# A three-layer graph attention kernel: layer A in three float32r products, two heads scaled on ScalarE, setup by small products, first and last six turns written out

## What is computed

```python
# layer 0 ("A"), one head of 256
Wh = x @ W;  e = leaky_relu(e_i[:, :, None] + e_j[:, None, :], 0.2)
attention = softmax(where(adj == 0, -1e9, e), axis=2)
x = layernorm(x + elu(attention @ Wh))
# layer 1, first part ("B", four heads of 128) and second part ("C", one head of 256)
mask = (adj > 0) | eye
h = elu(gat(x, mask, W1, att_src1, att_dst1, b1, concat=True))
h = gat(h, mask, W2, att_src2, att_dst2, b2, concat=False)
x = layernorm(x + h)
```

## Time and profile before

| | |
|---|---|
| median of 3 runs | 680.34 us (680.04 to 680.78) |
| the profiled execution | 680.93 us |
| its span, first to last instruction | 679.2 us |
| mean granted TensorE clock | 0.982 |
| busy: PE, DVE, ACT, POOL | 630.1, 598.4, 483.0, 456.0 us |
| bytes moved | 45.81 MB, mean 67 GB/s |

### The profile page before, as it was taken

How to read it: one execution, slowest core, us unless ns; L and a number is a source line. 1 busy time by engine, 2 the same in 40 slices (tenths; PEclk the granted TensorE clock), 3 DMA queues, 4 the chain that set the end, 5 groups by cost and what they waited for, 6 DMA issues and landing times. The chain is left out here.

```text
span 679.2 us, 17442 instructions
## 1 busy us (share of the span) xinstructions
PE 630.1 (93%) x4104; PEld 569.3 (84%) x4104; DVE 598.4 (88%) x2368; ACT 483.0 (71%) x1219; POOL 456.0 (67%) x810
## 2 busy tenths in 40 slices
PE   2468999999999999999999999999999999999883
PEld 1257889998999999889999999998999999999772
DVE  2567899999999999999999999999999999999852
ACT  1226777778777777787777777787777777787651
POOL 0125667777777777677777777777777777777742
PEclk9968999999999999999999999999999999999997
DMA  8112212112222222012222222112222222120000
GB/s 266 29 38 64 64 64 77 51 46 80 78 80 78 64 79 80 30 66 79 80 79 77 66 78 78 38 61 78 80 80 69 72 79 72 37 82 17 18 16 31
DMA packets 46868, 45.81 MB, mean 67 GB/s; under 512 B 2736, under 2 KB 46384, under 8 KB 46768
## 3 DMA queue, kind: packets, MB, share of 16 engines
q1 hardware_dynamic: 43936, 42.48, 19.6%
q10 hardware_dynamic: 2832, 2.23, 1.1%
HBM read 36.31 MB, written 8.39 MB: 66 GB/s over the span
## 5 line engine op out<-in xcount | busy, mean ns | idle before, releaser
L312 POOL TENSOR_SCALAR probB<-probB,rdenB 128x256 f32<-128x256 f32 x256 | 126.1, 505 | 74.3 <-DVE rdenB L618 73.9
L394 ACT ACTIVATE probB<-probB,shiftB 128x256 f32<-128x256 f32 x256 | 127.4, 499 | 24.2 <-DVE shiftB L587 20.7
L845 PE MATMUL PS<-probTB,VB 128*128 128x256 f32 x512 | 127.6, 382 | 0.0
L601 DVE SCALAR_TENSOR_TENSOR probB<-PS,VB,gatedB 128x256 f32<-128x256 f32 x256 | 111.5, 476 | 2.0 <-issue 0.4
L323 POOL TENSOR_TENSOR inlC<-hidT,inhC 128x512 fp32r<-128x512 f32 x64 | 82.2, 1285 | 45.0 <-ACT inhC L450 44.9
L559 DVE CUSTOM_DVE_ANT_0 gatedB<-PS,gate_bc 128x256 f32<-128x256 f32 x256 | 93.0, 417 | 7.7 <-PE PS L815 5.3
L845 PEld LDWEIGHTS PS<-probTB,VB 128*128 128x128 f32 x512 | 90.6, 192 | 8.7
L801 PE MATMUL PS<-WhB,inhB 128*128 128x260 f32 x256 | 81.6, 319 | 2.2 <-DVE inlB L632 2.1
L405 ACT ACTIVATE probTB<-PS 128x512 f32<-128x512 f32 x128 | 72.4, 591 | 8.3 <-PE PS L826 8.3
L294 POOL TENSOR_TENSOR y<-y,xres 128x512 f32<-128x512 f32 x32 | 41.2, 1288 | 51.0 <-DVE y L623 51.0
L801 PE MATMUL PS<-WhC,inhC 128*128 128x258 f32 x256 | 75.1, 293 | 0.2 <-issue 0.2
(11 more groups left out here) (98 smaller groups left out, 1631.7 us busy)
## 6 DMA issues: line engine op xcount, KB each, us to landing
xres<-in_x_dram SPq DMA_DIRECT2D x32, 256.0 KB, 2.7
xTin<-in_x_t_dram SPq DMA_DIRECT2D x32, 256.0 KB, 4.0
adj_in<-in_adj_dram SPq DMA_DIRECT2D x32, 256.0 KB, 4.3
adjT_in<-in_adj_t_dram SPq DMA_DIRECT2D x32, 256.0 KB, 3.1
out_dram<-res SPq DMA_DIRECT2D x32, 256.0 KB, 2.1
WB<-in_L_gnn_W_dram ACTq DMA_DIRECT2D x2, 256.0 KB, 5.8
WC<-in_L_gnn_W_dram ACTq DMA_DIRECT2D x1, 512.0 KB, 11.4
WA<-in_L_gnn_W_dram SPq DMA_DIRECT2D x1, 256.0 KB, 3.0
```

Source lines behind the costliest of these rows:

```text
L312: last = pool.tensor_scalar(B.prob[h][:, k, :], B.prob[h][:, k, :], B.rden[:, k, h:h + 1], 1.0, ALU.mult, ALU.mult)
L394: last = nc.scalar.activation(L.prob[h][:, k, :], L.prob[h][:, k, :], ACT.Exp, bias=L.shift[:, k, h:h + 1], accum_out=den[:, k, h:h + 1] i ...
L601: last = nc.vector.scalar_tensor_tensor(out=L.prob[h][:, k, :], in0=PS[b][:, (h % 2) * N:(h % 2 + 1) * N], scalar=L.V[:, k, h, 1:2], in1=L ...
L845: last = nc.tensor.matmul(PS[b][:, o:o + N], B.V[:, k, h, 2:B.F + 2], B.probT[h][:, k, :], start=(k == 0), stop=(k == NT - 1))
```

## The change

1. **A's projection** uses `project` as B and C do, with `A.Wh`, `A.Wl`, `A.inh`, `A.inl`: `high_a` (ACT) rounds xT, `low_a` (POOL) subtracts. SP's wait for a free xT buffer is on `low_a`.
2. **Heads 2 and 3 of B** are scaled on ACT (`scale_copy`), heads 0 and 1 stay on POOL (`scale`).
3. **Score columns** come from small PE products of the transposed weights, which are laid out and loaded too (`WT`), with two-column vectors (`score_products`), and one DVE copy each. The b1 and b2 rows are loaded once and spread by PE. Broadcast loads and the 28 DVE operations go. The column sums are taken with minus ones.
4. **Setup:** `load_table` (an exp on one element, ACT) and `warm_up` (four 128x128 products, PE) come first; the weight loads lie in the middle of SP's and ACT's lists.
5. **Order:** each queue is a written-out list `fill()`, then `body` for turns 6 to 30 (25 of them), then a written-out list `drain()`. Lags in the body are 0 and 1 for A, 2 to 4 for B, 4 and 5 for C. What a turn contains per batch is the same apart from 1 and 2.

Its core:

```diff
         def iterations(body):
-            for i in range(NB + 5):
+            for i in range(6, NB + 5 - 6):
                 body(Turn(i))
...
             def load_xT(t):
                 if active(t):
                     if t.at >= 2:
-                        for tile in range(NT):
-                            sp.wait_ge(A.s_lin[tile][0], t.this() - 2)
+                        sp.wait_ge(s_loA, t.this() - 2)
...
+            def low_a(t):
+                if active(t):
+                    pool.wait_ge(s_hiA, t.this())
+                    if t.later:
+                        for tile in range(NT):
+                            pool.wait_ge(A.s_lin[tile][0], t.last())
+                    pool.tensor_tensor(A.inl[:, :, :], xTin[t.at % 2][:, :, :], A.inh[:, :, :].bitcast(F32), ALU.subtract)\
+                        .then_inc(s_loA, 1)
...
+            def high_a(t):
+                if active(t):
+                    act.wait_ge(s_x[t.at % 2], t.loaded())
+                    if t.later:
+                        act.wait_ge(s_loA, t.last())
+                        for tile in range(NT):
+                            act.wait_ge(A.s_lin[tile][0], t.last())
+                    nc.scalar.activation(A.inh[:, :, :], xTin[t.at % 2][:, :, :], ACT.Copy).then_inc(s_hiA, 1)
...
+            def scale_copy(h, t):
+                if active(t):
+                    act.wait_ge(B.s_den[h], t.this())
+                    for k in range(NT):
+                        last = nc.scalar.activation(B.prob[h][:, k, :], B.prob[h][:, k, :], ACT.Copy,
+                                                    scale=B.rden[:, k, h:h + 1])
+                    last.then_inc(B.s_scaled[h], 1)
...
+            def score_products(L, b):
+                take_bank(b, [L.s_wab], Turn(0))
+                pe.wait_ge(s_vecs, 2)
+                pe.wait_ge(L.s_wtld, DMA)
+                first, n = {"A": (0, D // P), "B": (D // P, 1), "C": (D // P + B.H, D // P)}[L.name]
+                for k in range(L.KT):
+                    for h in range(L.H):
+                        o = 2 * (k * L.H + h)
+                        for q in range(n):
+                            v = 2 * (first + h + q)
+                            last = nc.tensor.matmul(PS[b][:, o:o + 2], L.WT[:, h + q, k * P:(k + 1) * P], vec[:, v:v + 2],
+                                                    start=(q == 0), stop=(q == n - 1))
+                last.then_inc(L.s_wa, 1)
```

```diff
+                load_biases(act)
+                load_vectors(act)
+                load_weights_T(act, A)
+                load_table()
+                high_a(b0)
+                round_weights(A)
+                load_weights_T(act, B)
+                values(A, 1, 1, b0)
```

PE's fill list, its beginning and its end, and the new turn:

```diff
+                warm_up(7, 4)
+                score_products(A, 7)
+                spread_b1(0)
+                project(A, 1, 0, 1, b0)
+                project(A, 0, 0, 6, b0)
+                spread(A, 0, 2, b0)
+                score_products(C, 0)
+                project(A, 0, 0, 5, b1)
+                project(A, 1, 0, 4, b1)
+                transpose_weights(A, 0, 7, b0)
...
+                weigh_head(0, 0, b2)
+                project(B, 0, 0, 5, b3)
+                project(B, 1, 0, 1, b3)
+                weigh_head(1, 0, b2)
+                weigh(A, 1, 3, b5)
+
             def body(i):
...
+                transpose_weights(B, 2, 2, t4)
+                spread(B, 0, 5, t3)
+                transpose_weights(B, 3, 1, t4)
+                weigh(A, 0, 4, t1)
+                weigh_head(2, 7, t4)
+                transpose_weights(C, 0, 0, t5)
+                weigh_head(3, 7, t4)
+                project(B, 0, 1, 2, t3)
+                project(A, 1, 0, 3, t0)
+                project(A, 0, 0, 5, t0)
+                project(B, 1, 1, 6, t3)
+                spread(A, 0, 7, t0)
+                weigh(C, 1, 1, t5)
+                weigh(C, 0, 3, t5)
+                transpose_x1(0, t2)
+                spread(B, 1, 4, t3)
                 project(C, 0, 0, 1, t4)
+                project(C, 1, 0, 3, t4)
+                transpose_weights(B, 0, 7, t3)
+                transpose_weights(A, 0, 2, t0)
+                transpose_weights(B, 1, 5, t3)
+                spread(C, 0, 6, t4)
+                weigh_head(0, 0, t3)
+                project(B, 0, 0, 5, t2)
+                project(B, 1, 0, 1, t2)
+                weigh_head(1, 0, t3)
+                weigh(A, 1, 3, t0)
```

The fill list of PE holds, beside the setup, for A six projections, spreads and transposes and eleven half weighings; for B four x1 transposes, 14 tile projections, six spreads, ten head transposes and ten head weighings; for C four tile projections, two spreads, one transpose and two half weighings. The drain list of PE ends:

```diff
+                weigh_head(2, 7, e1)
+                weigh_head(3, 7, e1)
+                transpose_weights(C, 0, 6, e2)
+                weigh(C, 1, 4, e2)
+                weigh(C, 0, 7, e2)
+                project(C, 0, 0, 6, e1)
+                project(C, 1, 0, 3, e1)
+                spread(C, 0, 0, e1)
+                transpose_weights(C, 0, 2, e1)
+                weigh(C, 0, 1, e1)
+                weigh(C, 1, 3, e1)
```

More of the change, by code:

```diff
@@ L227, in store, with fill @@
                     sp.dma_start(out_v[t.at], res[:, :, :]).then_inc(s_out, DMA)
+            def fill():
+                b0, b1, b2, b3, b4, b5 = Turn(0), Turn(1), Turn(2), Turn(3), Turn(4), Turn(5)
+                load_xT(b0)
+                load_weights(sp, A)
+                load_xT(b1)
+                load_weights_T(sp, C)
+                load_adj(b0)
+                load_xT(b2)
+                load_residual(b0)
+                load_weights(sp, C)
+                load_adjT(b0)
+                load_adj(b1)
+                load_weights(sp, B)
+                load_adjT(b1)
+                load_adj(b2)
+                load_adj(b3)
+                load_residual(b1)
+                load_residual(b2)
+                load_xT(b3)
+                load_adj(b4)
+                load_adjT(b2)
+                load_xT(b4)
+                load_residual(b3)
+                load_adjT(b3)
+                load_adj(b5)
+                load_residual(b4)
+                load_xT(b5)
+                load_residual(b5)
+                load_adjT(b4)
+                load_adjT(b5)
+                store(b0)
             def body(i):
@@ new lines, in body @@
+                exp(B, 2, t4)
+                exp(B, 3, t4)
+                scale_copy(2, t4)
+                scale_copy(3, t4)
+                elu_exp(0, 0, t4)
+                weights_copy(B, 2, 2, t4)
+                exp(C, 0, t5)
+                high_a(t0)
+                weights_copy(B, 3, 1, t4)
+                high_c(0, t4)
+                norm_first(1, 3, t1)
+                norm_first(0, 4, t1)
+                elu_exp(1, 7, t4)
+                weights_copy(C, 0, 0, t5)
+                elu_exp_first(t1)
@@ new lines, in body @@
+                top(C, 0, t5)
+                make_gate_b(t2)
+                shift(C, 0, t5)
+                values_b(0, 0, 5, t3)
+                values_b(1, 0, 1, t3)
+                logit(C, 0, 6, t5)
+                inverse_sum(A, 1, 3, t1)
+                elu(0, 0, t4)
+                maxima(B, 1, 5, t3)
+                maxima(B, 0, 5, t3)
+                inverse_sum(A, 0, 4, t1)
+                logit(B, 1, 5, t3)
+                logit(B, 0, 5, t3)
+                elu(1, 7, t4)
@@ L775, in column_sums, with warm_up @@
                                             stop=(k == C.KT - 1))
                 last.then_inc(s_cs, 1)
-                pe.wait_ge(s_fixc, 1)
-            def project_a(tile, b, t):
-                if active(t):
-                    take_bank(b, [A.s_v[tile][0]], t)
-                    if t.first:
-                        pe.wait_ge(A.s_wab, 2 * A.KT)
-                    pe.wait_ge(s_x[t.at % 2], t.loaded())
-                    for k in range(A.KT):
-                        last = nc.tensor.matmul(PS[b][:, 0:D + 2], xTin[t.at % 2][:, k, tile * P:(tile + 1) * P], A.W[:, k, 0, :],
-                                                start=(k == 0), stop=(k == A.KT - 1))
-                    last.then_inc(A.s_lin[tile][0], 1)
+            def warm_up(b, count):
+                for k in range(count):
+                    nc.tensor.matmul(PS[b][:, 0:P], ones[:, :], ones[:, :], start=True, stop=True)
```

1156 lines of the change are left out of this document (947 added, 209 removed).

## The result

The changed kernel took **696.02 us** (median of 4 runs, 688.65 to 697.75) against 680.19 us for the kernel before in the same session (679.93 to 680.78). The ratio of the two sets of runs, by their means, is 1.021, 95% interval 1.018 to 1.024. The forecast was 651, range 642 to 666, with a chance of 0.05 for slower.

The account below looks back on a forecast made before the run. PE was taken to bound the loop, DVE 0.84 us behind. Fill 88 + 25 turns x 18.85 (471.3) + remaining PE work 72.4 + rear loss 18.5 = 650.2, forecast as 651 us, range 642 to 666.

Parts of the forecast that it names:

- Step (5): Reordered queues and shorter lags: rounding and subtracting xT before A's products is hidden; uncovered, it costs 0.63 + 1.29 us once.
- The prediction's own sign of being wrong: In the loop turn, PE showing idle time behind ACT or DVE; also growing gates, or a fill ending past 94 us.
- The other half of (5): Steady loop: where PE is never idle, order alone is worth nothing; it counts only at the two ends.
- (1) A's projection: PE in each turn: 8 fp32 instructions (1.74 us) become 12 float32r ones (1.44), 0.30 off, giving 18.76.
- (2) ACT: ACT in each turn: four scaled copies at 0.45 us plus high_a at 0.63, 17.4 of 18.8 us, under PE.
- The rival that ACT is bound: Loop: scaled copies wait in ACT's queue for a reciprocal and hold PE; turn 21.5, time 717 us, chance 0.05.
- (3), (4) POOL and DVE: Loop turn: POOL falls from 14.27 to 13.6 us; DVE stays at 18.22, its slack falling from 0.84 to 0.54.
- the rival of stretched gates: Loop: DVE becomes the bound as gate operations stretch; turn about 19.1 to 19.3, time 657 to 662 us, chance 0.17.
- the 0.09 for a late DVE: Loop turn: 0.09 us added because PE can't hide every late DVE operation, giving 18.85; bounds 0 and 0.30.
- (6) Front: Start: first projection at 8.7 us, B's first products at 31.5; DVE 85% busy afterwards, fill ending at 88.
- the front loss: PE time lost before the steady loop: 29 us instead of 47.5.
- (7) Rear: End of the kernel: of 22 us lost, some 4.6 idle can be filled; 18.5 taken, bounds 15.5 and 22.

Follow-up runs that it names:

- after: The changed kernel as first measured, and its profile: 696.02 us median against 680.19 for the kernel before; the profiled execution took 688.65.
- e2: Changed kernel with the load of xT issued first in SP's turn instead of third, still behind the store: 658.54 us, ratio 0.970 to the kernel before.
- f2: Changed kernel with the load of xT issued last in SP's turn, behind adjT: 723.75 us, ratio 1.065 to the kernel before.
- g1: Changed kernel with high_a two places later in ACT's turn, SP's order unchanged: 674.49 us, ratio 0.993 to the kernel before.
- f1: Changed kernel with xT loaded first in SP's turn and A projected in fp32 again, without high_a and low_a: 667.73 us, ratio 0.983.
- e1: Changed kernel with SP loading xT of the next turn, ahead of this turn's store: 660.38 us, ratio 0.972 to the kernel before.
- f3: Kernel before with only A's projection changed to three float32r products, loads still a turn ahead: 718.24 us, ratio 1.057 to the kernel before.
- g2: Kernel before with A in float32r products and POOL's low_a moved later, behind scale(2): 754.71 us, ratio 1.110 to the kernel before.
- h2: Changed kernel with xT of the next turn loaded, and issued first in SP's turn: 662.44 us, ratio 0.975 to the kernel before.
- h1: Changed kernel with xT issued first in SP's turn and high_a two places later in ACT's turn: 658.81 us, ratio 0.971.

## Why the prediction was wrong

**Step (5) failed:** "this is early work on xT, which SP loads two ahead, and it is hidden". In the loop SP's queue loads xT ahead of nothing: the list that the change gives SP has load_xT(t0), and ACT's has high_a(t0), the same batch in the same turn. The prediction named the shorter lag ("A's chain starts in turn t0, not t1") in the sentence before and priced only the work that was added, at 0.63 + 1.29 once. It did not ask when the load is issued, behind what, and who is queued behind the wait. All numbers were there: about 4 us to landing, SP's queue held at the store until `normalise(C)`, ACT's list. The runs put a price on it: 1.06 us in the shown turn (19.81 against 18.75), 1.16 in the mean turn (20.04 against 18.89), 28.9 us for the 25 turns. Between after and e2 there are 31.0 us by the spans of the profiled executions (686.9, 655.9), of which the other 2.1 were there before B's first product, and 37.5 by the medians. The prediction's own sign of being wrong was met: PE showed idle time in the turn, 0.86 us of it, 0.81 in one wait for ACT.

**The other half of (5), "in a turn where PE is never idle order alone is worth nothing"**, assumes its own conclusion. f2, after, g1 and e2 differ in order alone and lie at 724, 696, 674 and 659.

By the other steps:

- *(1) A's projection* was right: 0.30 a turn predicted, 0.28 (ordinary) and 0.29 (mean) shown by f1 against e2. Twelve products lie 0.12 apart (two at 319.76 and 319.88).
- *(2) ACT*: 17.4 a turn predicted, 16.7 in e2. A scaled copy is 0.50 on the page, the upper bound, but four start in 1.59 us (331.70 to 333.29), 0.40 each, below the 0.45 taken. The rival that ACT is bound has the right sign and nearly the right shape (work behind a wait on ACT holds PE), with the wrong wait: the scaled copies waited for their reciprocal 2.3 us in the whole run. Its condition, over 2.6 us of ACT waits a turn, was met (3.21), by another wait than the one it named.
- *(3), (4) POOL and DVE*: DVE needs 17.8 in e2, not 18.22. gate_a fell from 569 to 420 ns in the mean, so the rival of stretched gates is refuted for this order. An ordinary turn of e1 and e2 is 18.75, as (1) alone says, so the 0.09 for a late DVE was not needed there. But the sum takes 25 mean turns, and the mean is 18.89, because a few turns are longer, as in the kernel before (19.06 and 19.14). That its 18.85 lies so near is luck.
- *(6) Front.* The first projection came at 12.77, not 8.7: the transposed weights of A landed at 9.0, not 5.5. The b1 row held PE for 2.0 us from 10.77, but only 0.3 of them beyond the split of WA, which ended at 12.50. B's first products came at 38.6, not 31.5, as late as before. The 22.8 us that were forecast from the first projection to B's first products are those of e2 (13.63 to 36.47); after took 25.8, with PE at half pace until about 24. And yet the front loss was 31.7 against 29, because DVE then ran at 96% (39.8 of 41.3 us from 38.7 to 80) where 85% was taken. Two errors of 7 us, in e2 of 5, nearly cancelled: that was luck.

```profile
9.01 1.84 PE L1467 MATMUL PS<-vec,WTA 128*128 128x2 f32 x8 [4.89 <-DMA WTA<-in_L_gnn_W_t_dram]
```

- *(7) Rear*: 22.8, not 18.5, and 87.1 us from the last projection of A in after, e1 and e2 alike, so it has nothing to do with the loop. PE idles 15.3 us of them (before 16.2 of its 72.1); only 0.9 of the 4.6 that could be filled was. The last 26.9 us run at a granted clock of 0.80.

With the load early, the change is worth what the forecast's sum gives, less its hope for the rear. In the profiled e2 the front loss is 29.6 (96.59 less 67) against 29, 25 turns of 18.89 are 0.9 more than forecast and the rear loss is 22.8 against 18.5: 650.2 + 5.8 = 656.0 for a span of 655.9. Its median of 658.5 against 651 is inside the range.

**The best version** is e2_xT_first: the change with one line moved, 658.54 us, 3.0% below the kernel before and 5.4% below the changed one.

## What to carry to other kernels

When a change shortens a lag, walk round the loop that it closes: when is the load issued, what does its queue wait for ahead of it, how long until it lands, what is queued behind the first instruction that waits for it, and does that lead back to the queue. If the sum passes the busiest engine's work, it is the new bound, however idle its engines are. A store that waits for the end of a chain does not belong ahead of a load that the beginning of the next one needs; issue such a load first, or a turn early.

## What was new about the hardware

- **A DVE operation on 4 columns with both inputs in SBUF was held for 0.96 us** beside POOL subtractions with SBUF inputs (0.15 to 0.17 alone), until the subtraction ended; one with an input in PSUM was not. The Trainium skill, SBUF — State Buffer, Who interferes with whom, says that a VectorE instruction with two SBUF inputs contends with a GpSimd instruction that reads SBUF, and that the contention is an exclusive lock on a shared pair of ports. The rows of f3 agree, to 0.06 us. Each took six times its usual 0.16 us. Two SBUF inputs are not needed for it: gate_a, with one (int32 to bf16), took 0.42 us in after and 1.33 at 366.55 in g2, beside POOL's 128x512 add from 366.31 to 367.59.
- **The place in SP's list changes the transfer itself**: the same 256 KB landed 2.9 us after issue when first of four loads and 4.1 when third, on top of 0.5 us for each place.
- **PE's pace in the first 35 us differs from execution to execution with the same lists**: half until about 17 us in e2, 24 in after and 34 in h2 (eight 257-column instructions in 1.97 or 3.77 us), which moved B's first product by up to 7.6 us (h1 against h2). The clock column reads 1.00 for all three in these stretches, so here the pace of the rows tells it and the column does not.
- **A longer wait can cost twice**: in six turns of f2 PE waited 1.9 to 3.6 us and then ran some 3.3 us at a granted clock of 0.50, which made each of these turns 1.5 us longer on top. In g2, where PE waits 1.9 us for `low_a` in every turn, eight of the 25 turns have such a stretch and take 22.7 us, the others 21.06 to 21.3.
- **The new order scatters more**: the four runs of after span 9.1 us, those of before 0.9. The variants that keep the change's lists for the start (e1, e2, f2, g1, h1, h2) span 3 to 7, with and without the wait for xTin. So the loop is not shown to be the reason; the point above may be part of it.
